# Attention stages: operand stores issued earlier on SyncE, and an exponent ahead of ScalarE's wait

## The reference

```
x = x + 0.5*moe(norm(x)); x = x + retention(norm(x)); x = x + 0.5*moe(norm(x))
x = x + 0.5*f(x)      # f1: attention, 32 heads of size 4, every key seen, then 8 experts
x = x + attn1(x)      # a1: attention, 16 heads of size 8, causal, rotary
x = x + 0.5*f(x)      # f2: as f1
x = x + 0.5*ternary_mlp(x); x = x + attn2(x)   # a2: as a1
x = x + 0.5*ternary_mlp(x); x = x + 0.5*binary_mlp(x); x = x + lion(x); x = x + 0.5*binary_mlp(x)
```

```
att = einsum('bqhd,bkhd->bhqk', q, k) * scale   # a1, a2: keys behind the query only
p = softmax(att, axis=-1)
o = einsum('bhqk,bkhd->bqhd', p, v)
```

## Time and profile before

| what | value |
|---|---|
| median of 3 runs | 2902.05 us (2901.3 to 2904.44) |
| the profiled execution's own time | 2903.42 us |
| its span, first to last instruction | 2901.7 us |
| mean granted TensorE clock | 0.948 of full speed |
| PE, DVE, ACT, POOL busy | 2618.3, 2288.0, 1871.3, 531.0 us |
| transfers | 120.80 MB, mean 42 GB/s |

### The profile page before, as it was taken

The page is one execution under the profiler, slowest core; times in us unless marked ns, Lnnn a source line. Parts: engine busy times, 40 slices in busy tenths (PEclk is TensorE's granted clock), DMA queues, the critical chain, the costliest instruction groups (busy, mean ns, idle before and its releaser), DMA issues. The chain is left out here.

```text
span 2901.7 us, 50700 instructions
## 1 busy us (share of the span) xinstructions
PE 2618.3 (90%) x19196; PEld 983.3 (34%) x19244; DVE 2288.0 (79%) x3516; ACT 1871.3 (64%) x3731; POOL 531.0 (18%) x847
## 2 busy tenths in 40 slices
PE   5998899899999999889978999999999789978778
PEld 2436644222222222623322222222227323335336
DVE  5456545799999998577858999999984878855993
ACT  2212322599999999546655999999995566655203
POOL 0000000310011110122313100111102222222771
PEclk9997999699999999989986999999999799989989
DMA  3220121400000000221114000000000311010000
GB/s 120 84 68 1 43 82 56 147 21 20 20 20 21 20 21 26 81 62 53 40 32 141 21 20 21 19 21 20 21 26 14 99 48 50 30 30 30 0 0 16
DMA packets 71996, 120.80 MB, mean 42 GB/s; under 512 B 16905, under 2 KB 44041, under 8 KB 68586
## 3 DMA queue, kind: packets, MB, share of 16 engines
q1 hardware_dynamic: 71754, 117.57, 12.7%
HBM read 94.19 MB, written 23.33 MB: 41 GB/s over the span
## 5 line engine op out<-in xcount | busy, mean ns | idle before, releaser
L1240 ACT ACTIVATE arena<-ps 128x512 f32<-128x512 f32 (+3 forms) x2816 | 1426.8, 571 | 234.2 <-PE ps L1045 168.7
L1367 DVE TENSOR_REDUCE arena<-ps 128x1 f32<-128x1024 f32 x1024 | 1172.3, 1214 | 24.9 <-PE ps L947 23.2
L947 PE MATMUL ps<-arena 61*128 61x512 bf16 (+4 forms) x2816 | 853.7, 381 | 44.7 <-DVE arena L1367 20.3
L1045 PE MATMUL ps<-arena 64*128 64x512 bf16 (+4 forms) x2768 | 826.9, 371 | 60.1 <-ACT arena L1240 32.2
L974 PE MATMUL ps<-arena 128*32 128x256 f32 (+2 forms) x9200 | 807.3, 423 | 0.4 <-POOL arena L1324 0.3
L1369 DVE CUSTOM_DVE_ANT_0 ps<-ps,arena 128x896 f32<-128x896 f32 (+7 forms) x512 | 376.3, 785 | 97.5 <-PE ps L947 93.3
L1045 PEld LDWEIGHTS ps<-arena 64*128 64x128 bf16 (+1 forms) x2816 | 184.9, 95 | 719.1 <-ACT arena L1240 576.2
L974 PEld LDWEIGHTS ps<-arena 128*32 128x32 f32 x9200 | 181.4, 108 | 422.4 <-ACT arena L1240 210.7
L947 PEld LDWEIGHTS ps<-arena 61*128 61x128 bf16 (+1 forms) x2816 | 193.0, 96 | 168.7 <-DVE arena L1367 83.2
L347 PE MATMUL ps<-xnT,moe_up 128*128 128x512 f32 x448 | 215.5, 606 | 0.0
L1293 POOL TENSOR_TENSOR arena<-arena,ones 16x128 bf16<-16x128 f32 x96 | 43.0, 448 | 903.7 <-ACT arena L1225 848.2
(11 more groups left out here) (243 smaller groups left out, 2509.5 us busy)
## 6 DMA issues: line engine op xcount, KB each, us to landing
arena<-m_w SPq DMA_DIRECT2D x40, 256.0 KB, 3.1
arena<-f_q SPq DMA_DIRECT2D x60, 144.0 KB
arena<-f_k SPq DMA_DIRECT2D x180, 48.0 KB
arena<-in_w SPq DMA_DIRECT2D x4, 2048.0 KB
arena<-a_q SPq DMA_DIRECT2D x14, 576.0 KB
arena<-a_k SPq DMA_DIRECT2D x42, 192.0 KB
a_q<-arena SPq DMA_DIRECT2D x44, 96.0 KB, 2.0
a_k<-arena SPq DMA_DIRECT2D x44, 96.0 KB, 2.0
```

The source lines that it names most:

```text
L947: last = nc.tensor.matmul(at[:, k0 // CHUNK, 0:n], score_rows(Qop[par], j, slice(q0, q0 + P)), score_rows(Kop[par], j, slice(k0, k0 + n)), ...
L1045: nc.tensor.matmul(ps[:, ring_bank(item), off:CHUNK], shifted_rows(Kop[par], j, slice(kb * P, (kb + 1) * P)), shifted_rows(Qop[par], j, sl ...
L1240: nc.scalar.activation(pr[:, (at % 2) * 4 + j, off:CHUNK], ps[:, ring_bank(item), off:CHUNK], ACT.Exp).then_inc(s.ex, 1)
L1367: nc.vector.tensor_reduce(top, src, AXX, ALU.max).then_inc(s.sread, 1)
```

## The change

Three edits. In SP's program all stores of chunk 2, and in a full stage those of chunk 3 too, are issued ahead of the wait for batch 0's stores and of unit 1's loads. `put_max` is split into `store_max` and `load_max`, and in a causal stage the stores of chunk 3 go between the two. In ACT's program one exponent of a column of ones, written to a new one-word buffer `spare`, is computed ahead of the wait for batch 1's stores. `spare` is carved between `mr` and `ms`.

```
             mr = c(P)
+            spare = c(1)
             ms = c(2 * 3 * P, BF16).rearrange("p (n a t) -> p n a t", n=2, a=3)
...
-                def put_max(u, par, qc):
-
+                def store_max(u, qc):
                     sp.wait_ge(s.mps, 2 * u + qc + 1)
                     sp.dma_start(mt[qc]..., ms[0:16, qc, :, :]).then_inc(max_stored[qc], 16)
+
+                def load_max(u, par, qc):
                     sp.wait_ge(max_stored[qc], 16 * (u + 1))
                     for side in range(SIDES):
...
+                def put_max(u, par, qc):
+                    store_max(u, qc)
+                    load_max(u, par, qc)
...
                 store_cut(1)
+                store_cut(2)
+                if full:
+                    store_cut(3)
                 sp.wait_ge(s.qst0, N_CUT)
                 sp.wait_ge(s.kst0, N_CUT)
                 sp.wait_ge(s.kneg, 2)
                 load(1, 1)
                 if full:
-                    store_cut(2)
-                    store_cut(3)
                     put_max(0, 0, 0)
                 else:
-                    put_max(0, 0, 0)
-                    store_cut(2)
+                    store_max(0, 0)
                     store_cut(3)
+                    load_max(0, 0, 0)
...
+                nc.scalar.activation(spare, ones[:, 0:1], ACT.Exp)
                 act.wait_ge(s.qst1, N_CUT)
                 act.wait_ge(s.kst1, N_CUT)
                 loops(unit)
```

## The result

The changed kernel takes 2885.48 us (median of 4 runs, 2880.62 to 2887.91) against 2903.24 us for the kernel before on the same chip (4 runs, 2901.3 to 2904.88): a ratio of 0.994 [0.9927, 0.9952]. The profiled execution took 2887.91 us (span 2886.2), 15.5 less than the profiled execution before.

The account below looks back on a forecast made before the run. DVE's maxima were taken to pace the full stages, and ACT's late first exponent, waiting for last-issued stores, to hold the causal ones. 5.1 + 5.1 + 1.2 + 1.0 = 12.4 us gave 2891.0 profiled, 2889.7 us forecast, range 2884 to 2897.5.

Parts of the forecast that it names:

- the causal mechanism: In a1 and a2, ACT's first exponent waits for stores issued last, then loads its table; removing both gains 5.1 us each.
- 12.3 forecast: Sign in a1: SP issues the maxima's load some 12.3 us behind their store instead of 10.6, chunk 3's stores between.
- the forecast's best case: All four attention stages at their upper bounds: 5.3 + 5.8 + 2.1 + 2.5 = 15.7 us, giving 2886.4.
- clock bonus: Rival, chance 0.07: without its pause PE may clock up earlier, full stages lose all stalls, 1 to 3 us of clock; 2883 to 2886.
- I take 1.0 us for the queue: Causal stages: the maxima's load stands behind chunk 3's stores on three DMA engines, delaying PE's first score 1.0 us, at most 3.75.
- The 2.60 of the earlier trace: From f2: 2.60 us from issue of the maxima's load to PE's first score, used to place the causal first scores.
- 5.1 and 5.1: Gains at ACT's first exponent: a1 from 1262.69 to 1257.6, a2 from 2326.34 to 2321.2, 5.1 us each.
- 1.2 + 1.0: Gains read on DVE in the full stages: f1 1.2 us (0 to 2.1), f2 1.0 us (0 to 2.5).
- maxima 1.0 us earlier give some 0.3 more: In f1, the maxima's store ending 1.0 us earlier adds some 0.3 us to the 0.9 from hiding the table load.
- The drain: At ACT's table switches, the skill's rule gives 2.66 us with drain; the forecast took the trace's 1.28 us and no drain.
- Maxima late: Rival, chance 0.12: ring queue at its slowest in the causal stages, a1's exponent at 1262.5, 0.2 us gained there; about 2900.
- Displaced buffers: Rival, chance 0.04: buffers moved 4 bytes slow the 512 causal maxima of 785 ns; at 60 ns each +31, 2920 us.

Follow-up runs that it names:

- causal order alone: Kernel before plus SP's new store order in the causal stages only, no early exponent: 2892.64 us, 0.9964 against 2903.13 before.
- full order alone: Kernel before plus SP's new store order in the full stages only, no early exponent: 2903.0 us, 0.9996 against 2903.13 before.
- repeat: The changed kernel run again unaltered: 2883.51 us, 0.9936 against the kernel before.
- kernel with the pause filled: Changed kernel with chunk 3's stores behind the maxima's load, plus 14 throwaway matmuls in PE's pause before the causal exponents: 2890.84 us against 2901.57 before, 0.9964.
- the order alone: Changed kernel without the early exponent and its buffer, SP's new order in all stages: 2892.64 us, 0.9965 against 2903.13 before.
- two kernels with the old full order: Kernel before plus only the early exponent (2900.39 us, 0.9995), and kernel before plus only the new causal store order (2892.64 us, 0.9964).
- the wide loads: Changed kernel with causal units' operands loaded by 12 transfers a side without the outer dimension of three: 2885.22 us, 0.9945 against the kernel before.
- the kernel with the busy full prologue: Changed kernel plus one throwaway matmul behind each of tasks 16 to 25 of a full prologue: 2887.86 us, 0.9952 against the kernel before.
- the buffer moved away: Changed kernel with `spare` carved behind the last cut buffer, so nothing is displaced: 2885.78 us, 0.9941 against the kernel before.

## Why the prediction was right, and where it was not

**Right: the causal mechanism.** Both causal first exponents were bound by stores issued last, and moving those ahead of the wait between store and load of the maxima frees them. The causal order alone brings 10.5 of the 17.8 us, the full order alone nothing, and putting chunk 3 back behind the maxima's load loses 9.2. SP, ACT and PE look in a1 as foretold: 12.9 us between store and load (12.3 forecast), the exponent 0.77 us behind the score (0.8), released by PE.

**In the range, but not by the forecast alone.** The median of 2885.48 lies below the forecast's best case, 2886.4, and inside the 2883 to 2886 of the clock bonus. The range holds it because half of that case had been taken in. The parts that follow were off by up to 2.2 us each, in both directions.

**Mis-sized: the charge on the first score, and where that score was.** The step "I take 1.0 us for the queue" set PE's first score 0.2 us later in a1 and 0.7 in a2. Against the first causal maximum it came at the same distance in a1 and 0.1 us later in a2. With chunk 3 ahead of it, the load of the maxima took 2.5 to 2.6 us from its issue to the score in the change and its repeat, with chunk 3 behind it 2.5: chunk 3 held back nothing that can be seen. The 2.60 of the earlier trace rows, from which the sum took this time, fits by chance: in f1 and f2 PE's first score stands 10.29 or 10.30 us behind the second 16 tasks wherever PE's tasks are left alone, whether the load comes 3.2 or 7.7 us behind them, so the row shows no more than an upper bound. And the first score that the sum started from, 1256.62, is PE's second; from the real one to the exponent it was 6.47 and 7.00 us. With both, the gain at the exponent is 5.7 and 6.1 instead of 5.1 and 5.1: of the 1.6 us between them 0.8 are the charge and 0.8 the missing records.

**Left out of the sum: the clock.** The pause of PE behind its first scores costs 0.7 and 1.5 us more in the 12 us that follow, in the pair of profiled executions. (Measured against the causal stages of the kernel with the full order alone, which take 14.0 and 14.2 us there, it is 1.5 and 1.8.) The forecast saw this (the rival "clock bonus", chance 0.07, "1 to 3 us of clock") and gave it no term. That was the heaviest error, for it was not a rival but a part of the forecast's own mechanism: whoever removes the pause removes its second price. The kernel with the pause filled shows it to be the clock, 12.3 against 14.0 us. It also accounts for why the edits don't add up: with the order alone, the table load leaves PE a pause of its own.

**Too high: the full stages.** 1.2 + 1.0 were forecast, 0.4 + 0.9 came by the landmarks, and f2's 0.9 is partly chance, as its 1.29 us stall was absent from two kernels with the old full order. The maxima did come 0.9 us earlier in f1, as assumed (6.06 us behind the second 16 tasks instead of 6.99). The step that did not hold is "maxima 1.0 us earlier give some 0.3 more" and its basis: over all runs that leave PE's tasks alone, the maxima's load ranges from 3.2 to 7.7 us behind the start of the second 16 tasks, and the first exponent stands at 11.10 to 11.12 wherever the table is loaded early or was left in place, at 12.38 to 12.39 in f1 where it isn't. So it is bound by the tasks, not by the maxima. And hiding the table did not leave f2's stall of 1.17 us but one of 1.64.

**The corrections in numbers.** 12.4 + 0.8 (missing records) + 0.8 (no queue charge) + 0.7 + 1.5 (clock) - 0.9 (full stages) = 15.3 us, the sum of the rows, against 15.5 between the two profiled executions. That these two are so close is partly chance, since stretches that no edit touches differ too: from the copy in a1 to f2's second 16 tasks the change takes 2.4 us less than the kernel before, from f1 to a1 and from f2 to a2 2.4 more. The medians differ by 17.8. For the remaining 2 us I can name two sources, not their shares. One is the scatter of the rows before, 1.6 us in the causal stages as said above. The other is the start of f1, ahead of any changed code, which wanders. SP's first transfer there (L143) starts at 507.88 us in the kernel before and at 500.57 with the full order alone. Over the 14 profiled executions it lies between 500.57 and 508.09 us. The rest stays open.

**The drain.** The forecast took the rows: 1.28 us for a table load and nothing behind it. The rule of the Trainium skill (ScalarE: Activation LUTs, What ACT_TABLE_LOAD costs) is 2.66 us a switch, 1283 ns for the load and about 1380 for a drain. With the order alone the exponent starts 0.02 us behind the end of the table load (1257.08 + 1.28, then 1258.38), and the switch delays it by 1.28 us in a1 and in a2 (2.05 instead of 0.77 us behind PE's first score). No drain is seen behind the load here; what might stand ahead of it would be hidden in ACT's wait.

**The other rivals.** Maxima late: the load was indeed 12.9 to 13.5 us behind the store, but the price is small, as the score tasks bind PE nearly as late (the wide loads show less than a microsecond between them). It isn't always so: in the kernel with the busy full prologue, whose causal stages are those of the change, the load came 14.6 and 15.6 us behind the store and the first score waited 1.7 and 1.9 us for it. What delayed it there is open. Displaced buffers: refuted, 784 ns against 785, and the buffer moved away changes nothing.

## What to carry to other kernels

When an engine's first work of a stage waits for a store, look at what its issuing queue stood waiting for before it: a wait between a small store and its load is free room for everything that is ready. Price a pause of TensorE twice, once for its length and once for the clock behind it, and take this from windows laid behind the pause; here it made 2.2 of 15.3 us. And two edits that end the same wait are not worth the sum of their parts: test each alone and both together before giving up one that alone shows nothing. And before you read a distance of less than a microsecond from PE's first row to another engine's, compare the number of matmul records with that of their weight loads: with 48 of 2816 missing it was off by 0.38 us here.

## What the runs showed of the hardware that I had not expected

- SyncE's issuing slows behind a load confined to few DMA engines: four issues took 4.42 us instead of 1.88, and one of 0.31 took 2.10. Going behind such a load is no cheaper for the queue than going ahead of it.
- TensorE, busy for 3.00 of 3.00 us in stretch after stretch of some 12 us (552.81 to 564.81), stayed at a granted clock of 0.50 in the kernel with the busy prologue.
- The maxima's store, 16 rows of 384 bf16, took 9.5 and 7.7 us from its issue to that of the load which waits for it, even with the wide load, in a1 at 118 to 158 GB/s on 0.78 to 0.80 of the engines.
- The start of f1, ahead of anything changed, varied by 7.5 us between the profiled executions.
